# Attention pooling on one core: keys loaded as eight small transfers per tile in a window of four, and another order at the front

## What is computed

```python
feat = jnp.concatenate([qe, k, qe - k, qe * k], axis=-1)   # qe: q repeated for each key
h = feat @ W1 + b1                                         # 512 -> 64
h = jnp.where(h >= 0, h, alpha[0] * h)
a = (h @ W2 + b2)[..., 0]                                  # 64 -> 1
a = jnp.where(mask == 0, jnp.float32(NEG), a)
w = jax.nn.softmax(a, axis=-1)
return jnp.einsum('bl,bld->bd', w, k)
```

## Time and profile before

| | |
|---|---|
| median of three timed runs | 1017.25 us (1008.7, 1017.25, 1024.19) |
| the profiled execution's own time | 1018.95 us |
| its span | 1017.0 us |
| mean granted TensorE clock | 0.983 |
| busy: PE, DVE, POOL, ACT | 83%, 76%, 65%, 52% |

### The profile page before, as it was taken

How to read it: one execution, slowest core, us unless ns; L and a number is a source line. 1 busy time by engine, 2 the same in 40 slices (tenths; PEclk the granted TensorE clock), 3 DMA queues, 4 the chain that set the end, 5 groups by cost and what they waited for, 6 DMA issues and landing times.

```text
span 1017.0 us, 55327 instructions
## 1 busy us (share of the span) xinstructions
PE 847.9 (83%) x25216; PEld 559.4 (55%) x25216; DVE 769.4 (76%) x1143; ACT 532.8 (52%) x1281; POOL 656.3 (65%) x401
## 2 busy tenths in 40 slices
PE   0769888988888898889889889888887888888896
PEld 0435555655555565556555556555555555545564
DVE  2879777878788778787787888777886777867771
ACT  0355545655555565555555555555554555545552
POOL 0657666767667676676666667667666667657661
PEclk9899999999999999999998999999999999989999
DMA  8844766667776766786675777766677676667630
GB/s 253 322 148 138 268 204 212 233 201 239 253 236 228 238 206 230 238 270 211 229 231 185 236 266 238 232 223 226 204 242 257 211 230 209 217 225 233 213 103 11
DMA packets 67017, 222.45 MB, mean 219 GB/s; under 512 B 25312, under 2 KB 33504, under 8 KB 66784
## 3 DMA queue, kind: packets, MB, share of 16 engines
q1 hardware_dynamic: 66784, 218.92, 65.0%
HBM read 214.57 MB, written 4.33 MB: 215 GB/s over the span
## 4 chain that ended last, share of the span: by engine, by line
PE 40%; DVE 16%; DMA 15%; issue 13%; ACT 8%; SPq 7%; POOL 0%; DVEq 0%; ACTq 0%; POOLq 0%
PE hP L431 22%; DMA keys<-in_r_k 9%; PE poolP L472 9%; DVE act L348 9%; PE scoreP L460 7%; ACT act L289 6%; DVE keysT L340 5%; DMA probs_scratch<-expd 5%; SPq L160 3%; SPq L211 2%; ACT expd L313 2%; PE poolP L480 1%; DVE neg_max L361 1%; DVE logits L355 1%; DMA w2c<-in_L_rec_W 1%
## 5 line engine op out<-in xcount | busy, mean ns | idle before, releaser
L289 ACT ACTIVATE act<-hP,biast,al 128x200 f32<-128x200 f32 x1024 | 459.5, 515 | 329.6 <-PE hP L431 325.9
L340 DVE STREAM_TRANSPOSE keysT<-keys 128x768 f32<-128x768 f32 (+1 forms) x512 | 510.1, 997 | 60.4 <-DMA keys<-in_r_k 60.3
L431 PE MATMUL hP<-keysT,weff 32*64 32x200 f32 x16384 | 475.5, 344 | 30.3 <-issue 23.5
L232 POOL TENSOR_TENSOR weff<-qX,wp 128x1024 f32<-128x1024 f32 x128 | 244.0, 1906 | 324.3 <-PE hP L431 300.7
L431 PEld LDWEIGHTS hP<-keysT,weff 32*64 32x64 f32 x16384 | 310.2, 133 | 186.2 <-issue 113.1
L348 DVE TENSOR_TENSOR act<-hP,act 128x400 f32<-128x400 f32 x512 | 283.9, 554 | 146.8 <-ACT act L289 143.0
L236 POOL TENSOR_TENSOR weff<-weff,wk 128x1024 f32<-128x1024 f32 x128 | 303.2, 2369 | 10.0
L472 PE MATMUL poolP<-keys,pool_w 128*16 128x128 f32 x6400 | 244.6, 276 | 22.7 <-issue 21.2
L472 PEld LDWEIGHTS poolP<-keys,pool_w 128*16 128x16 f32 x6400 | 173.4, 97 | 98.1 <-issue 93.0
L460 PE MATMUL scoreP<-act,w2win 128*16 128x200 f32 x2048 | 151.3, 341 | 81.3 <-DVE act L348 70.3
L271 POOL TENSOR_TENSOR pool_w<-probs_k,own_b 128x400 f32<-128x400 f32 x128 | 111.3, 870 | 15.7 <-DMA probs_k<-probs_scratch 7.9
(11 more groups left out here) (35 smaller groups left out, 40.9 us busy)
## 6 DMA issues: line engine op xcount, KB each, us to landing
keys<-in_r_k SPq DMA_DIRECT2D x128, 832.0 KB, 5.5
keys<-in_r_k SPq DMA_DIRECT2D x128, 768.0 KB, 5.2
probs_scratch<-expd SPq DMA_DIRECT2D x32, 100.0 KB, 3.7
masks<-in_r_mask SPq DMA_DIRECT2D x128, 12.5 KB
probs_k<-probs_scratch SPq DMA_DIRECT2D x128, 12.5 KB
out_rows<-pooled SPq DMA_DIRECT2D x128, 8.0 KB
keys<-in_r_q SPq DMA_DIRECT2D x4, 256.0 KB, 5.0
act<-in_L_rec_W SPq DMA_DIRECT2D x4, 128.0 KB, 6.1
```

The source lines that it names most:

```text
L232: g_.tensor_tensor(weff[:, n % 2, :, :, :], qX[:, n, :, :].unsqueeze(3).broadcast_to([P, BQ, CD, H]), wp[:].unsqueeze(1).broadcast_to([P, ...
L289: a_.activation(act[:, k, a, :], hP[:, 2 * (p % HSETS) + a % 2, 0:L], ACT.Identity, bias=biast[:, n, k, a:a + 1], scale=al[:]).then_inc(t_ ...
L340: v_.transpose(keysT[:, n % TBUF, j0 * D:j1 * D], keys[:, n % SLOTS, j0 * D:j1 * D]).then_inc(keysT_done, 1)
L431: mm = t_.matmul(hP[H * r:H * r + H, 2 * (p % HSETS) + a % 2, 0:L], weff[QP * a:QP * a + QP, n % 2, w, c, :], kT[QP * a:QP * a + QP, :, c, ...
```

## The change

1. A tile is loaded as eight transfers: seven of three rows (192 KB) and one of four (256 KB). Transfers are numbered through, i = 8n + x; transfer i is counted on semaphore i % 4, and SP issues it only when transfer i - 4 has landed.
2. The waits for DVE's transposes in `paced_part` are gone; `part_done` stays ahead of a tile's first transfer. At the front the wait of tile n for tile n - 2 is gone.
3. Each piece of DVE's transposes waits for the two transfers that hold its rows.
4. SP writes the probabilities behind the sixth transfer of its step (n % 4 = 0), and waits for that and reads them back behind the second transfer of the next step; the masks are issued behind the fifth transfer of that step.
5. Front: the parameters are loaded first, then queries, W1 and tile 0. DVE transposes the queries ahead of the fold, and makes `w2win` right behind it; half of tile 0 stands ahead of the biases and half behind, then `nshift`, then half of tile 1. PE's wait for `fold` 11 moves from ahead of the first layer to ahead of the first `second_layer`, the one for `consts_done` into `add_parts`; ACT's `fill(0)` moves behind its first two pairs.

```diff
-LOADS = 2
-LOAD_CUT = [0, 12, J]
+LOAD_CUTS = [0, 3, 6, 9, 12, 15, 18, 21, J]
+PARTS = len(LOAD_CUTS) - 1
+WINDOW = 4
...
             def load_part(n, x):
-                at = slice(LOAD_CUT[x] * D, LOAD_CUT[x + 1] * D)
-                sp.dma_start(keys[:, n % SLOTS, at], k_tiles[n][:, at]).then_inc(keys_in[n % SLOTS], 16)
+                i = n * PARTS + x
+                ge(sp, keys_in[i % WINDOW], i // WINDOW * 16)
+                at = slice(LOAD_CUTS[x] * D, LOAD_CUTS[x + 1] * D)
+                sp.dma_start(keys[:, n % SLOTS, at], k_tiles[n][:, at]).then_inc(keys_in[i % WINDOW], 16)
...
             for n in range(STEPS):
-                def paced_part(x):
-                    if SLOTS <= n + AHEAD < TILES:
-                        behind = PIECES * (n + 1) + 2 + x * PIECES // LOADS
-                        sp.wait_ge(keysT_done, min(behind, PIECES * TILES))
-                        load_part(n + AHEAD, x)
...
+                for x in range(PARTS):
+                    if SLOTS <= n + AHEAD < TILES:
+                        if x == 0:
+                            sp.wait_ge(part_done, n + AHEAD - SLOTS + 1)
+                        load_part(n + AHEAD, x)
+                    g = (n - 0) // GT - 1
+                    if n % GT == 0 and x == 5 and 0 <= g < GROUPS:
+                        sp.wait_ge(exp_done, g + 1)
+                        ge(sp, poolw_done, (g - 1) * GT)
+                        sp.dma_start(probs_dram[g % 2], expd[:, g % 2, :]).then_inc(probs_out, 16)
+                    g = (n - 1) // GT - 1
+                    if n % GT == 1 and x == 1 and 0 <= g < GROUPS:
+                        sp.wait_ge(probs_out, (g + 1) * 16)
+                        for t in range(GT):
+                            sp.dma_start(probs_k[:, g % 2, t, :], probs_tiles[g % 2, t]
+                                         ).then_inc(probs_in[GT * (g % 2) + t], 16)
+                    g = n // GT - 1
+                    if n % GT == 1 and x == PARTS // 2 and 0 <= g < GROUPS - 2:
+                        sp.wait_ge(scores_read, g + 1)
+                        load_mask(g + 2)
...
             def transpose_piece(n, piece):
+                for x in range(PARTS):
+                    if CUTS[piece] <= LOAD_CUTS[x] < CUTS[piece + 1]:
+                        i = n * PARTS + x
+                        dve.wait_ge(keys_in[i % WINDOW], (i // WINDOW + 1) * 16)
                 if piece == 0:
-                    dve.wait_ge(keys_in[n % SLOTS], (n // SLOTS + 1) * 16 * LOADS)
                     ge(dve, main_done, PAIRS * (n + 1 - TBUF))
```

More of the change, by code:

```diff
@@ L104, in attention_pooling @@
         poolP = ps("poolP", [P, 512])
-        keys_in = [sem(f"keys_in{x}") for x in range(SLOTS)]
+        keys_in = [sem(f"keys_in{x}") for x in range(WINDOW)]
         mask_in = [sem(f"mask_in{x}") for x in range(2)]
@@ L161, in load_mask @@
                                  mask_rows[g, c]).then_inc(mask_in[g % 2], 16)
+            sp.dma_start(al[:], alpha.rearrange("(a b) -> a b", b=1).broadcast_to([P, 1])).then_inc(params_in, 16)
+            sp.dma_start(b2c[:], b2.rearrange("(a b) -> a b", b=1).broadcast_to([P, 1])).then_inc(params_in, 16)
+            for r in range(2):
+                sp.dma_start(b1c[H * r:H * r + H, :], b1.rearrange("(a b) -> a b", b=1)).then_inc(params_in, 16)
+                sp.dma_start(w2c[H * r:H * r + H, :], W2).then_inc(params_in, 16)
             for a in range(QUADS):
@@ L169, in _ @@
             load_keys(0)
[L170 to L174, removed]
             for n in range(1, SLOTS):
-                if n > 2:
-                    sp.wait_ge(keys_in[n - 2], 16 * LOADS)
                 if n == 3:
@@ L197, in _ @@
[L197 to L212, removed]
@@ L213, in _ @@
-                for x in range(LOADS // 2 + 1, LOADS):
-                    paced_part(x)
+                    g = (n - 0) // GT - 1
[9 more added lines that the diff above has]
+                                         ).then_inc(probs_in[GT * (g % 2) + t], 16)
@@ L296, in _ @@
             a_.preload_act_table(ACT.Exp)
-            act_e.wait_ge(fold, 11)
-            fill(0)
+            act_e.wait_ge(bias_done, QUADS + 1)
             for n in range(STEPS):
@@ L307, in _ @@
                 scale_pair(PAIRS * n)
+                if n == 0:
+                    act_e.wait_ge(fold, 11)
+                    fill(0)
                 g = n // GT - 1
@@ L367, in _ @@
             v_.memset(neg[:], NEG).then_inc(zeroed, 1)
+            dve.wait_ge(q_in, 16 * QUADS)
+            v_.transpose(qX[:].rearrange("p (t y) w c -> p t (w c) y", y=QP), q_sb).then_inc(qx_done, 1)
             dve.wait_ge(w1_in, 16 * QUADS)
@@ L379, in _ @@
             v_.tensor_scalar(wq[:], wq[:], sgn[:], None, ALU.mult).then_inc(fold, 1)
[L380 to L383, removed]
             v_.tensor_scalar(b1s[:], b1c[:], sgn[:], None, ALU.mult).then_inc(fold, 1)
@@ L390, in _ @@
             mm.then_inc(fold, 1)
+            for piece in range(2):
+                transpose_piece(0, piece)
             dve.wait_ge(bias_mm, 1)
@@ L397, in _ @@
             v_.tensor_scalar(biast[:], bias[:], al1[:], None, ALU.mult).then_inc(bias_done, 1)
+            for piece in range(2, 4):
+                transpose_piece(0, piece)
+            dve.wait_ge(shift_mm, 1)
+            v_.tensor_scalar(nshift[:], scoreP[:, 0:GROUPS], b2c[:], -1.0, ALU.add, ALU.mult).then_inc(fold, 1)
             for piece in range(2):
                 transpose_piece(1, piece)
-            dve.wait_ge(shift_mm, 1)
-            v_.tensor_scalar(nshift[:], scoreP[:, 0:GROUPS], b2c[:], -1.0, ALU.add, ALU.mult).then_inc(fold, 1)
             for n in range(STEPS):
@@ L455, in second_layer @@
                 pe.wait_ge(act_done, PAIRS * n + 2 * k + 2)
+                if n == 0 and k == 0:
+                    pe.wait_ge(fold, 11)
                 if n % GT == 0 and k == 0:
@@ L477, in add_parts @@
             def add_parts(g):
+                pe.wait_ge(consts_done, GT)
                 pe.wait_ge(parts_done, GT * (g + 1))
@@ L505, in _ @@
             mm.then_inc(shift_mm, 1)
-            pe.wait_ge(fold, 11)
-            pe.wait_ge(consts_done, GT)
             for n in range(STEPS):
```

2 lines of the change are left out of this document (removed).

## The result

The changed kernel is slower: a median of 1119.29 us (four runs, 1113.72 to 1122.91) against 1020.72 us for the kernel before on the same chip; the ratio is 1.1045, 95% interval 1.0933 to 1.1157. The profiled execution took 1122.91 us, its span is 1121.0 us. I had forecast 970 us.

The account below looks back on a forecast made before the run. Key loading through the window of four was to bound the kernel: 72.2 us of filling, 29.5 groups of 29.1 (858.5), 2.9 landing, 34.1 tail and 1.95 around it gave 970 us; range 947 to 1045.

Parts of the forecast that it names:

- part 3: SP's key loading: at most four transfers, 786 KB, under way, so their landing time sets the pace, 29.1 us a group.
- L: Time from a 192 KB key transfer's issue to its landing in the window of four; taken as 2.9 us, bounds 2.4 to 4.4.
- rival (c): Key loading: small transfers land later under load, waiting for all 16 engines; at L = 3.5, 1088 us; chance 0.25.
- 8 issue edges and 6 hops: Longest path through a group's 32 key transfers: 0.46 us per issue, 2.93 per landing, plus read-back, masks, output: 29.1 us.
- (a): Main forecast for key loading: the window paces at L of 2.75 to 3.04, 29.1 us a group, 970 us; chance 0.37.
- The filling: Start of key loading: 80 transfers fill ten places in 58.6 us, masks add 5.3, ending at 72.2 us.
- Place 0: First of the ten key places; claimed to come free at about the time they are all filled, 72.2 us.
- PE's start: Front: with the new load order PE begins tile 0 at some 26.2 us instead of 33.88; gain taken as 7.5 us.
- SP's 108.9 us of standing still: SP's 32 waits for the probabilities' write to land; nearly vanish with four key transfers between write and read-back.
- a late tile costs less with waits by piece: DVE's transposes: each piece waits only for its own rows, instead of the first carrying the whole wait; no size given.
- The removed waits on the transposes cost nothing by themselves: SP's key loading: dropping its waits for DVE's transposes costs 0 us, since `part_done` still holds the place.
- part 2: SP between the probabilities' write and read-back: its 108.9 us of waits nearly vanish; a 1 to 2 us delay is covered.

Follow-up runs that it names:

- the one with the lowest median: Changed kernel with a window of sixteen transfers and the read-back behind the fourth transfer of its step instead of the second: 953.5 us, ratio 0.9389 to the kernel before.

## Why the prediction was wrong

**The step that failed** is part 3, "So L = 4.4 - 1.5 = 2.9 us"; measured, L is 3.5 us. It took the landing of a transfer that had little beside it, scaled it to size, and put it into a window that always has three neighbours. Alone, such a transfer is even quicker than I said: behind the masks, at 518.4 us, one lands in 2.5 us (its DMA issue line, then that of one issued at 522.4 us behind three others):

```profile
keys<-in_r_k SPq DMA_DIRECT2D x1, 192.0 KB, 2.5
...
keys<-in_r_k SPq DMA_DIRECT2D x1, 192.0 KB, 4.4
```

But a window that is kept full gives each transfer neighbours. Two stretches near it (columns as in the earlier trace rows), and the landing of the transfer issued in front of it, at 520.9 us:

```profile
522.00:523.00 1.00, 0.84 (x28) 0.56 (x24) 0.57 (x1) 1.00 (x3) 1.00 (x1) 1.00 1.01 310
525.50:526.50 1.00, 1.00 (x50) 0.71 (x34) 0.05 (x1) 0.42 (x1) 1.00 (x2) 1.00 0.07 25
```
```profile
keys<-in_r_k SPq DMA_DIRECT2D x1, 192.0 KB, 5.5
```

In the first stretch the DMA engines were full and moved 310 GB/s, not the 425 of the earlier trace rows. At that rate the data of 192 KB take 0.63 us. My estimate for a transfer behind three others is then up to 2.5 + 3 x 0.63 = 4.4 us, and the median of 3.5 lies between that and 2.5. It is no upper bound: the run's longest landing is 6.1 us, and the one of 5.5 us ends at 526.4, after a stretch in which the engines' share was 0.07, about one engine of 16, while the rest moved nothing. This fits the mechanism of rival (c), a transfer that waits for its last engine. So clear a case is rare here, some 3 in 100 landings by a count over the records; how the 0.6 us that L grew by divides between queueing and late engines isn't told apart, and what made that engine late isn't shown.

With 3.5, my own sum gives 8 issue edges and 6 hops of 3.53, 32.7 us, against 33.2 measured. The path was the forecast's (a); that a small transfer lands later under load was rival (c), which named L = 3.5 and 1088 us.

**The sum** was 153 us short in span. The filling ended at 83.2 instead of 72.2 us, by the same landing (20 hops of 0.6), 11. Place 0 came free only at 94.6, as the first read-back stood behind the filling, another 11. I had put these two at "about" the same time without following the first group's probabilities through SP's queue. From there to the last key issue, at 1082.5 us, the 29.5 groups took 988 us instead of 858.5, some 130: 33.5 a group, a little over the 33.2 between exponentials.

**Right.** PE's start at 26.11 us; that SP's 108.9 us of standing still would go; that the path of window and SP issues sets the pace, shown by windows of 2, 4 and by six-row transfers, whose groups it gives, with each run's own median landing, as 45.1, 32.7 and 32.7 us for 48.2, 33.2 and 33.2. For a window of six it gave 26.3 for 29.8, until the write's landing was put in. That a late tile costs less with waits by piece fits (DVE's waits rose by 161 us, the groups by 92), but no run tests it alone. **Wrong beside L.** "The removed waits on the transposes cost nothing by themselves": with long rows they are worth 7%. With short rows in a window of sixteen they are worth nothing; in the window of four, which paces the transfers itself, they were not tried. The write's landing stays in SP's path as soon as the window is large enough (52.8 us with eight), which part 2 left out. The fit of the Trainium skill ("DMA: Bandwidth & Descriptors", Anatomy of one DMA) gives 2.45 us for 192 KB. It is stated there for transfers that GpSimd issues, and these are SP's; the trace's 2.5 us for a lone one agrees with it all the same. What failed is what the neighbours add. The rule of 1 MiB or more for a DMA (same page, Rules for kernel authors) is for the highest bandwidth, and no run here tests it: eight 192 KB transfers in flight, 1.6 MB, gave the 235 GB/s that the other engines could use, four gave 202.

**Range and chances.** The window had no reserve, as rival (c) said, at 20 us for each 0.1 us of L. The uncertainty of L, 2.4 to 4.4 by my own bounds, spanned far more than the range that I gave, and a quarter of the chance was too little for the side to which neighbours in flight push L.

## What to carry to other kernels

A window of transfers is a throughput limit: bytes in flight over the landing time under that very load, less whatever else the issuing queue does; take the landing at the planned depth, not of a lone transfer, and leave a reserve, since here going from four to eight moved the ratio from 1.10 to 0.95 and from eight to sixteen did nothing. When a queue that issues in order stands still for one landing, split the issue from the wait and put other work between; here, with the old transfers and pacing, the new front and the waits by piece, that came to 5%. Before removing a wait that "costs nothing", ask what it spreads out.

## What the hardware showed unexpectedly

- A 192 KB transfer landed in 2.5, 3.5, 4.1 and 4.4 us (medians) at windows of 2, 4, 6 and 8. In the window of eight, by the number of key transfers still under way when it was issued (none to seven), the medians are 2.5, 2.5, 3.4, 3.9, 4.4, 4.6, 4.6 and 4.9 us, counted over the trace's records: the first neighbour adds nothing, the next two most.
- Rows of 1.5 KB cost the DMA engines little more time for their bytes than rows of 6 KB: shares of 0.75 and 0.75 at 235 and 236 GB/s (window eight; two transfers paced). It isn't nothing: the median packet of 1.5 KB takes 65 ns and one of 6 KB 234, counted over the changed kernel's and the kernel before's records, which is 378 against 420 GB/s for 16 engines. In the changed kernel a share of 0.68 moved 202 GB/s, in the kernel before 223.
- The length of rows and their bunching go with PE's waits for issue: ahead of the first layer and the pooling they were 91.2 us with 6 KB rows unpaced, 67.6 with 3 KB rows, 33.8 with 1.5 KB rows in a window of eight, 42.8 with 6 KB rows paced.
- The mean granted clock over the 30 groups was 0.81 at window two, 0.97 in the changed kernel and 1.00 in the one with the lowest median; PE's busy time for the same work was 980.9, 797.1 and 777.3 us. It doesn't go by PE's idle time alone: PE was busy 80% of these groups in the changed kernel at 0.97, but 86% at 0.96 with long rows unpaced, and 83% at 0.93 in the kernel before with eight transfers.
